# A 256-node graph network: one-hots of the last layer moved behind the next sums' remainder, a new order of the first stage, attention keys made as rows, fillers near the end

## What is computed

```python
x = _layernorm(x + _L0_gnn_ref(...))   # relational conv (3 relations) + gate over queries, twice
x = _layernorm(x + _L1_gnn_ref(...))   # plain graph conv
x = _layernorm(x + _L2_gnn_ref(...))   # relational attention, 4 heads, then 1 head
x = _layernorm(x + _L3_gnn_ref(...))   # relational conv, 34 relations, then a graph conv

# gate of the first layer: what the first stage prepares
qg = jnp.einsum('blf,gf->blg', q, Wg[:, F:]) + bg
# attention of the third layer
xr = jnp.einsum('nd,rdf->rnf', x, W)
qi = xr[etype, dst] @ q
kj = xr[etype, src] @ k
alpha = jax.nn.leaky_relu(qi + kj, NEG_SLOPE)
# last layer
mean = agg.reshape(N_REL, n, -1) / jnp.maximum(cnt, 1.0).reshape(N_REL, n, 1)
h1 = jnp.einsum('rni,rio->no', mean, W_rel) + x @ W_root + b_rgcn
```

## Time and profile before

| | us |
|---|---|
| median of three runs | 1136.41 (1133.11 to 1136.69) |
| the profiled execution, its time | 1134.0 |
| the profiled execution, its span | 1132.3 |
| PE busy in the span | 1078.2 (95%) |
| DVE busy | 768.5 (68%) |
| ACT busy | 572.1 (51%) |
| POOL busy | 179.9 (16%) |

### The profile page before, as it was taken

The page is one execution under the profiler, slowest core; times in us unless marked ns, Lnnn a source line. Parts: engine busy times, 40 slices in busy tenths (PEclk is TensorE's granted clock), DMA queues, the critical chain, the costliest instruction groups (busy, mean ns, idle before and its releaser), DMA issues.

```text
span 1132.3 us, 17627 instructions
## 1 busy us (share of the span) xinstructions
PE 1078.2 (95%) x7440; PEld 894.1 (79%) x7440; DVE 768.5 (68%) x1082; ACT 572.1 (51%) x602; POOL 179.9 (16%) x96
## 2 busy tenths in 40 slices
PE   7999999999999999999999889899999999999987
PEld 5899986545699965457689889759999999999974
DVE  6993855888743158885364665557788888888852
ACT  0433225888433268883233544225666656666630
POOL 2334702555100025551000000000000000000000
PEclk9999999999999999999999899999999999999999
DMA  9034276111044381120244004409777777777720
GB/s 295 11 99 154 85 235 197 57 57 57 1 167 168 121 241 57 57 57 3 93 157 167 29 1 168 163 1 320 244 238 246 248 252 242 248 234 248 241 85 28
DMA packets 82323, 163.47 MB, mean 144 GB/s; under 512 B 4035, under 2 KB 60127, under 8 KB 81951
## 3 DMA queue, kind: packets, MB, share of 16 engines
q1 hardware_dynamic: 80736, 151.86, 39.8%
q0 software_dynamic: 1504, 10.44, 3.6%
HBM read 158.64 MB, written 0.80 MB: 141 GB/s over the span
## 4 chain that ended last, share of the span: by engine, by line
PE 68%; DVE 19%; ACT 5%; issue 4%; DMA 1%; POOL 1%; SPq 0%; DVEq 0%; ACTq 0%; POOLq 0%
PE PS L1012 12%; PE PS L714 7%; PE PS L870 7%; PE PS L730 5%; PE PS L461 4%; PE PS L636 4%; DVE Wlo L1822 3%; PE PS L612 3%; PE PS L1026 3%; PE PS L995 3%; PE PS L474 3%; ACT Whi L1346 3%; PE PS L543 2%; PE PS L770 2%; PE PS L931 2%
## 5 line engine op out<-in xcount | busy, mean ns | idle before, releaser
L1822 DVE TENSOR_TENSOR Wlo<-W,Whi 128x2304 fp32r<-128x2304 f32 x68 | 173.7, 2556 | 43.5 <-ACT Whi L1346 43.4
L1346 ACT CAST Whi<-W 128x2304 fp32r<-128x2304 f32 x68 | 144.4, 2125 | 0.0
L1012 PE MATMUL PS<-Whi,Mhi 128*128 128x384 f32 x408 | 139.6, 342 | 3.5 <-DVE Mlo L1851 3.5
L1012 PE MATMUL PS<-Wlo,Mhi 128*128 128x384 f32 x408 | 136.6, 335 | 0.0
L1012 PE MATMUL PS<-Whi,Mlo 128*128 128x384 f32 x408 | 136.5, 335 | 0.0
L433 POOL TENSOR_TENSOR PRDP<-arena 128x1024 f32<-128x1024 f32 x48 | 114.6, 2388 | 113.7 <-PE PS L730 86.5
L714 PE MATMUL PS<-QH,SEL 128*128 128x512 f32 x384 | 115.7, 422 | 5.2 <-ACT xT L1186 1.4
L1207 ACT ACTIVATE arena<-PS 128x1024 f32<-128x1024 f32 x96 | 98.5, 1026 | 23.5 <-PE PS L714 23.5
L714 PEld LDWEIGHTS PS<-QH,SEL 128*128 128x128 f32 x384 | 64.8, 188 | 55.1 <-DVE PRD L1592 21.3
L1207 ACT ACTIVATE PS<-PS 128x1024 f32<-128x1024 f32 x96 | 97.9, 1020 | 2.6 <-PE PS L714 2.6
L1012 PEld LDWEIGHTS PS<-Whi,Mhi 128*128 128x128 f32 x408 | 76.7, 188 | 8.3 <-DVE Mlo L1851 8.3
(11 more groups left out here) (276 smaller groups left out, 2391.4 us busy)
## 6 DMA issues: line engine op xcount, KB each, us to landing
W<-in_L_rel SPq DMA_DIRECT2D x68, 1152.0 KB, 5.8
W<-in_W_rel SPq DMA_DIRECT2D x6, 2304.0 KB, 8.5
W<-in_W SPq DMA_DIRECT2D x6, 2304.0 KB, 8.5
arena<-in_qU SPq DMA_DIRECT2D x96, 128.0 KB, 2.6
W<-in_WqT SPq DMA_DIRECT2D x4, 2304.0 KB, 9.8
W<-in_W_root SPq DMA_DIRECT2D x2, 2304.0 KB, 13.6
W<-in_WgT SPq DMA_DIRECT2D x2, 2304.0 KB, 9.0
QH<-QH POOLq DMA_DIRECT2D x2, 1536.0 KB, 10.4
```

The lines of the kernel that those rows point to most:

```text
L1012: mm = pe.matmul(PS[:, 4 + s % 2, 0:HALF], MS[a][mb][:, k, j * P:(j + 1) * P], WS[b][w % 3][:, k, :], start=n == 0, stop=n == 17)
L1346: nc.scalar.copy(WS[0][w % 3][:], W[(FIRST34 + r) % 2][:, :, q * HALF:(q + 1) * HALF]).then_inc(w_hi, 1)
L1822: V.tensor_tensor(WS[1][w % 3][:], W[(FIRST34 + r) % 2][:, :, q * HALF:(q + 1) * HALF], WS[0][w % 3][:].bitcast(F32), ALU.subtract).then_i ...
```

## The change

It has four parts. First, in the last layer, the one-hots with `j = 1` are made in s = 0 of the pair behind the remainder of part 2, not in s = 3 ahead of it. Second, the first stage: the bias comes from eight matmuls in the rounded format with 33 rows (`BG` holds the rounded bias in row 0 and its remainder in row 32, `ROWS2` ones in these rows); ACT and POOL make `BG` and `ROWS2`; the first half of the query product comes ahead of the counts; relation 2 is counted behind the halves; and DVE's list is put in another order. Third, `queries_keys` holds `qk1` as weights (8 columns) and streams 256 columns of the transposed tiles, DVE negates rows into `qkR`, `spread_keys` spreads a row of it, and `turn_queries` turns the rows into `qkN`; `turn_rows(2)` comes ahead of `queries_keys(1)`. Fourth, `keep_busy(12, 7)` stands behind the `pe.Else` block.

```diff
@@ tensor engine, first stage @@
-            pe.wait_ge(consts, 2)
-            pe.wait_ge(bg_in, 16)
-            for at in range(4 * 3):
-                pe.matmul(PS[:, at // 2, (at % 2) * THIRD:(at % 2 + 1) * THIRD], ones[0:1, :],
-                          biasN[0:1, 5, at % 3 * THIRD:(at % 3 + 1) * THIRD], start=at % 2 == 0, stop=False, skip_group_check=True)
+            pe.wait_ge(bg_ready, 1)
+            for u in range(2):
+                for bank, at, f, n in ((0, 0, 0, 512), (1, 0, 512, 256), (1, 256, 0, 256), (2, 0, 256, 512)):
+                    pe.matmul(PS[:, 3 * u + bank, at:at + n], ROWS2[:], BG[:, f:f + n], start=at == 0, stop=False,
+                              skip_group_check=True)
+            pe.wait_ge(q_in[0], 16)
+            for q in range(3):
+                pe.wait_ge(w_in[0] if q == 2 else first_in[q], 16)
+                mm = natural3(qT[0], W[0], last=True, thirds=[q])
+            mm.then_inc(q_done, 1)
             for c in range(EC):
...
@@ tensor engine, attention @@
-                for t in range(NT):
-                    at = (t * R3 + r) * 2 * HEADS1
-                    for k in range(KC):
-                        mm = pe.matmul(PS[:, 3, at:at + 2 * HEADS1], XT[:, r, k, t * P:(t + 1) * P], qk1[:, k, :],
-                                       start=k == 0, stop=k == KC - 1)
-                return mm
+                for k in range(KC):
+                    mm = pe.matmul(PS[0:2 * HEADS1, 3 + r // 2, (r % 2) * NODES:(r % 2 + 1) * NODES], qk1[:, k, :], XT[:, r, k, :],
+                                   start=k == 0, stop=k == KC - 1)
+                mm.then_inc(qk_done, 1)
+
+            def turn_queries():
+
+                for c in range(R3 * NT):
+                    r, t = divmod(c, NT)
+                    mm = pe.transpose(PS[:, 6, 2 * HEADS1 * (R3 * t + r):2 * HEADS1 * (R3 * t + r + 1)],
+                                      qkR[:, c * P:(c + 1) * P], ident[0:2 * HEADS1, 0:2 * HEADS1])
+                mm.then_inc(rows_turned, 1)
...
+                    for r in range(R3 if l == 0 else 0):
+                        mm = pe.matmul(PS[:, 4 - h % 2 * 2 + r // 2, (r % 2) * NODES:(r % 2 + 1) * NODES],
+                                       ident[0:2 * HEADS1, HEADS1 + h:HEADS1 + h + 1].to_broadcast([2 * HEADS1, P]),
+                                       qkR[:, r * NODES:(r + 1) * NODES], start=True, stop=True)
@@ tensor engine, end @@
+            keep_busy(12, 7)
             to_turned(4, hN, ready=lambda t: pe.wait_ge(h1_copied, t + 1)).then_inc(h_turned, 1)
@@ gpsimd, first stage @@
+            pool.wait_ge(consts, 2)
+            pool.wait_ge(bg_hi, 2)
+            nc.gpsimd.tensor_tensor(BG[32:33, :], biasN[32:33, 5, :], BG[32:33, :].bitcast(F32), ALU.subtract).then_inc(bg_ready, 1)
@@ vector engine, attention @@
-                    dve.wait_ge(qk_done, 1)
-                    V.tensor_scalar(qkN[:], PS[:, 3, 0:NT * R3 * 2 * H].rearrange("p (t r h) -> p t r h", t=NT, r=R3),
-                                    -1.0, None, ALU.mult).then_inc(qkn_copied, 1)
+                    dve.wait_ge(qk_done, 2)
+                    V.tensor_scalar(qkR[:, 0:2 * NODES], PS[0:2 * H, 3, :], -1.0, None, ALU.mult).then_inc(qkr_copied, 1)
+                    dve.wait_ge(qk_done, 3)
+                    V.tensor_scalar(qkR[:, 2 * NODES:], PS[0:2 * H, 4, 0:NODES], -1.0, None, ALU.mult).then_inc(qkr_copied, 1)
+                    dve.wait_ge(rows_turned, 1)
+                    V.tensor_copy(qkN[:], PS[:, 6, 0:NT * R3 * 2 * H].rearrange("p (t r h) -> p t r h", t=NT, r=R3)
+                                  ).then_inc(qkn_copied, 1)
@@ vector engine, last layer @@
                         if s == 0 and p:
                             sums_lo(p, 2)
+                            if p + 1 < PAIRS34:
+                                pair_onehots(p + 1, 1)
...
-                        elif p + 2 < PAIRS34:
-                            pair_onehots(p + 2, s - 2)
+                        elif s == 2 and p + 2 < PAIRS34:
+                            pair_onehots(p + 2, 0)
```

More of the change, by code:

```diff
@@ L133, in build @@
         qkN = sb("qkN", [P, NT, R3, 2 * HEADS1])
+        qkR = put("qkR", [2 * HEADS1, R3 * NODES], F32, 36)
         RC = sb("RC", [P, 2, NODES])
@@ L375, in _ @@
             nc.gpsimd.tensor_copy(iotab[:], iota1[:]).then_inc(consts, 1)
-            pool.dma_start(biasN[:, 5, :], A["bg"].partition_broadcast(P)).then_inc(bg_in, 16)
+            pool.dma_start(biasN[0:33, 5, :], A["bg"].partition_broadcast(33)).then_inc(bg_in, 16)
+            then(nc.gpsimd.memset(ROWS2F[:], 0.0))
+            then(nc.gpsimd.memset(ROWS2F[0:1, :], 1.0))
+            nc.gpsimd.memset(ROWS2F[32:33, :], 1.0).then_inc(rows2_set, 1)
+            pool.wait_ge(rows2_set, 1)
             then(nc.gpsimd.iota(relid[:], pattern=[[1, R34]], base=0, channel_multiplier=0,
@@ L577, in _ @@
                     mm.then_inc(cnt_summed, 1)
-            pe.wait_ge(q_in[0], 16)
-            for q in range(3):
-                pe.wait_ge(w_in[0] if q == 2 else first_in[q], 16)
-                mm = natural3(qT[0], W[0], last=True, thirds=[q])
-            mm.then_inc(q_done, 1)
+            pe.wait_ge(e_ready, R3)
+            pe.wait_ge(half_read, 1)
+            for s in range(NT):
+                for c in range(EC):
+                    mm = pe.matmul(PS[:, 6, s * NODES:(s + 1) * NODES], S1[:, c, s * P:(s + 1) * P], E[0][:, c, :],
+                                   start=c == 0, stop=c == EC - 1)
+            mm.then_inc(cnt_summed, 1)
+            pe.wait_ge(consts, 2)
             pe.wait_ge(cnt_copied, 2)
@@ L587, in _ @@
             mm.then_inc(deg_spread, 2)
-            counts(2, 0, bank=6)
             pe.wait_ge(q_in[1], 16)
@@ L904, in spread_keys @@
                         pe.wait_ge(score_done, u0 + 2 * h - 2)
-                    for c in range(R3 * NT):
+                    for r in range(R3 if l == 0 else 0):
+                        mm = pe.matmul(PS[:, 4 - h % 2 * 2 + r // 2, (r % 2) * NODES:(r % 2 + 1) * NODES],
+                                       ident[0:2 * HEADS1, HEADS1 + h:HEADS1 + h + 1].to_broadcast([2 * HEADS1, P]),
+                                       qkR[:, r * NODES:(r + 1) * NODES], start=True, stop=True)
+                    for c in range(R3 * NT if l == 1 else 0):
                         r, s = divmod(c, NT)
@@ L936, in _ @@
                     spread_keys(h)
+                    if l == h == 0:
+                        turn_queries()
                 keep_busy(30 if l == 0 else 52, 7)
@@ L1121, in third_hi_first @@
                 nc.scalar.copy(WH[(w + 1) % 3][:], third_turned(W[m % 2], w % 3)).then_inc(wr_hi, 1)
-            act.wait_ge(cnt_summed, 1)
-            third_hi_first(0)
-            third_hi_first(1)
+            act.wait_ge(rows2_set, 1)
+            nc.scalar.copy(ROWS2[:], ROWS2F[:]).then_inc(bg_hi, 1)
+            act.wait_ge(bg_in, 16)
+            nc.scalar.copy(BG[:], biasN[0:33, 5, :]).then_inc(bg_hi, 1)
             for t in range(NT):
@@ L1128, in _ @@
                 if t == 0:
+                    third_hi_first(0)
+                    third_hi_first(1)
                     act.wait_ge(x_in, 32)
@@ L1446, in _ @@
             dve.wait_ge(chunk_ready, EC)
+            then(V.scalar_tensor_tensor(out=ekey[:, 0, :], in0=keyf[:, 2, :], scalar=2.0, in1=keyf[:, 1, :], op0=ALU.is_equal, op1=ALU.mult))
+            onehot(E[0], ekey[:, 0, :]).then_inc(e_ready, R3)
             for h in range(2):
@@ L1453, in _ @@
                 then(V.scalar_tensor_tensor(out=low, in0=high, scalar=-STEP, in1=both, op0=ALU.mult, op1=ALU.add))
+                dve.sem_inc(half_read, 1)
             V.tensor_tensor(CNT[:, 0], CNT[:, 0], NRM[:, 1], ALU.add).then_inc(cnt_copied, 1)
             V.tensor_tensor(CNT[:, 1], CNT[:, 1], NRM[:, 2], ALU.add).then_inc(cnt_copied, 1)
-            then(V.scalar_tensor_tensor(out=ekey[:, 0, :], in0=keyf[:, 2, :], scalar=2.0, in1=keyf[:, 1, :], op0=ALU.is_equal, op1=ALU.mult))
-            onehot(E[0], ekey[:, 0, :]).then_inc(e_ready, R3)
-            onehot(E[1], keyf[:, 1, :]).then_inc(d1_ready, 1)
             def normalise_counts(n):
```

22 lines of the change are left out of this document (15 added, 7 removed).

## The result

The changed kernel takes **1117.5 us** (median of 4 runs, 1116.7 to 1119.2), the kernel before on the same chip 1135.3 (4 runs, 1133.1 to 1136.7): ratio 0.984, 95% interval 0.981 to 0.987. The forecast was 1122.5 with a range from 1117.5 to 1128, so the sign held and so did the mechanisms of the last layer and the first stage, while the attention was priced wrongly: 17.8 us were gained where 12.7 were forecast. The profiled execution of after took 1118.25 us against 1134.0, and has 15.8 of these 17.8.

A forecast was written before the change was run, and what follows sets the result against it. PE was taken to bound the last layer, PE and DVE the first stage, a DVE and ACT chain the attention. First stage -4.5, attention -1.7, last layer -7.0, fillers +0.5: -12.7 from 1135.2, so 1122.5 us, range 1117.5 to 1128.

The forecast's parts named there:

- Last layer, forecast -7.0: Last layer: moved one-hots let `Mlo` come 0.72 us earlier, ending PE's stall; 0.47 x 15 = 7.0 us gained.
- The 0.04 a pair: Last layer: average loss counted per pair because `Ylo` is next to be late, with 0.1 to 0.15 us left.
- the first rival: Last layer: `Ylo` binds instead, by 0.25 us or more a pair; layer gains 3.8, time 1125.7 us; chance 0.15.
- First stage, forecast -4.5: First stage: DVE decides and `Tlo` starts at 81.3, 4.4 us earlier; gain rounded to 4.5 us.
- PE's -5.3: First stage, PE: bias -10.6, new bias and later start +2.5, half clock level paid by the query product +2.8.
- Attention, forecast -1.7: Attention: scores start earlier, by the middle of 2.8 and 0.8 us, rounded down to 1.7.
- If half a relation and half the spread fall in it, 1.3 + 0.7 are lost: Attention: loss from PE's lower clock level, leaving 0.8 us of the 2.8 us gain.
- The reading that a busy PE keeps its clock: Attention: by the Trainium skill's page the relations keep the upper level; term -2.8, time 1.1 us lower.
- raised the level by 1.2: Whole kernel: base put at 1135.2 us, halfway between the profiled 1134.0 and the runs' median, 2.4 above it.
- Fillers, forecast +0.5: End: twelve fillers cannot fill the gap, cost 1.35 us, and give 0.7 to 1.0 back in the product; net +0.5.
- The third rival: All parts at their good ends: -6 - 2.8 - 7.6 - 1.2 = -17.6, time 1117.6 us; chance 0.10.
- The fifth rival: Last layer: `Ylo` late in every pair; at 0.6 further behind, 9 us lost, time 1138.5 us; chance 0.03.

The follow-up runs named there:

- e11: The changed kernel with the one-hots of the last layer in their old place; 1125.6 us, ratio 0.990 to the kernel before.
- e5: The changed kernel with all eight one-hots of a pair behind the next sums' remainder, ahead of `Ylo`; 1130.4 us, ratio 0.994 to the kernel before.
- e1: The kernel before with only the last layer's one-hots with j = 1 moved; 1127.4 us, ratio 0.990 to the kernel before.
- e2: The kernel before with the attention's part alone; 1133.2 us, ratio 0.996 to the kernel before.
- e3: The kernel before with the first stage's part alone; 1134.3 us, ratio 0.998 to the kernel before.
- e10: The changed kernel with the attention's order and query sums as before; 1125.8 us, ratio 0.990 to the kernel before.
- e4: The changed kernel without the twelve filler matmuls behind the Else block; 1119.3 us, ratio 0.984 to the kernel before.

## Why the prediction missed

**Last layer, forecast -7.0, measured -7.7** (6.8 by medians). Every step stood: the wait of `half_product` for `Mlo` is gone, it returns with the one-hots (e11), and `Ylo` is what comes next. The 0.04 a pair taken off for it was not lost. e5 shows how near the first rival was: 0.72 us more at this place cost 0.70 a pair.

**First stage, forecast -4.5, measured -4.9 at `Tlo`** (4.2 to 5.4, mean 4.9, in nine other executions with the new stage), and -5.6 where the gates begin, since PE waited 0.6 less for a transfer ahead of them. In e1 and e2, with the old stage, the gates begin 1.7 and 1.6 later than in the profile of before, so that one was on the good side here as well; on average over three executions with the old stage and ten with the new one the gates come 7.0 sooner. The engine that decides, DVE, was right, as were its pieces: 6.75 for `E0`, 37.99 for the start of its list, 0.69 for the product that had met POOL. PE's -5.3 was right too, by its first later product (63.2, 5.5 earlier). The timed runs of e3 show less (-2.7 by the ratio, interval -0.9 to -4.5, and -1.7 by the medians). In its trace the attention is 3.0 slower than in the profile of before, by the clock, and the end 3.2, of which 2.8 are the second gap.

**Attention, forecast -1.7, measured -2.7 against the profile of before, -4.8 in the traces on average: the term that failed.** By the times it is -2.8 to -4.4 alone (e2) and -7.0 when it is undone (e10, with the second gap). Two steps of it were wrong. First, "If half a relation and half the spread fall in it, 1.3 + 0.7 are lost": nothing of it was. In each of eleven executions the phase took the 12.7 of the sum of pieces. The bias matmuls, busy throughout with one row of 128 at 1.2 GHz, were the wrong relative; they follow an idle PE, these follow full products, and that this is the reason is argued, not tried. The margin was small: the fall did come, 1.6 us behind the scores' start in the changed kernel and at that start in e2. The reading that a busy PE keeps its clock, which the prediction had set beside it at -2.8, would have been right for this execution. Second, and worth more, the size of the old phase: "Now the phase lasts from 619.06 to 634.52, 15.5 us" is one execution, and a lucky one. In three others it is 18.3 to 19.7, so against these the phase gains 6.1 (mean 18.8 less 12.7), against all four 5.3. Behind it DVE and ACT's chain gives a little back: from the first matmul of `rows` to the first turned probabilities the old code takes 64.1, 68.4, 67.1 and 66.9 us, the new one 61.5 in nine of eleven executions (the others 63.1 and 63.2), 4.8 less on average. The rows themselves had a warning: the earlier trace rows show relation 3 at 2.88 and then the spread at twice its price, so the clock fell in the middle of the phase, and where it falls need not be the same each time. The forecast raised the level by 1.2 for the runs and put none of it where it belonged.

The old attention and a slow end go together. From the last scatter to the last product it takes 28.7, 29.7 and 31.9 us with the old attention and no fillers (before, e1, e3), 27.2 and 26.7 with the new one (e2, e4). In e3 the second gap accounts for 2.83 of it; without that the five are 28.7, 29.7, 29.1 and 27.2, 26.7, so about 2.2 us remain. They are in the product, which takes 17.87 to 18.30 in the first three, where the granted clock is 0.50 for 6.8 to 10.2 us ahead of it and in it, and 15.72 in the other two, where it is 0.50 for 3.4. Why that should hang on the attention is not shown; it stays open.

**Fillers, forecast +0.5, measured about +1.9.** That they stand behind the gap and can't fill it was right; that the product recovers by them was not. The product takes 15.72 with them and 15.72 without (e4), and the step that priced them at 1.35 us assumed the upper level, where they ran at the lower one (2.74). In the seven executions with the whole new attention and the twelve fillers the end takes 28.3 to 29.6 us, mean 28.9, against 27.0 for e2 and e4. Timed runs can't separate it (1119.3 without; 1117.5 and 1118.8 with).

**The sum.** By the traces: first stage -5.6, attention -4.8, the faster end that goes with it -2.2, last layer -7.7, fillers +1.9: -18.4, where -17.3 and -17.8 were measured (with the first stage's average of -7.0 it would be -19.8); averages over a few executions leave that much open. Of the 5 us by which the forecast was short, the attention makes 3.1 and the end that goes with it 2.2; the other terms, -1.1, -0.7 and +1.4, nearly cancel. The third rival, everything at the good ends, gave 1117.6 and had a chance of 0.10; that it met the time is luck, since its parts are wrong (an attention at -2.8, fillers that save 1.2). The fifth rival's price holds a slip: at 0.38 us behind its point the time is just 1135.2, and it takes 0.6 to be 0.3% above. Nothing else hangs on it.

## What to carry to other kernels

A phase in which TensorE works at less than its full array differed here by 4 us between executions with the same code; profile such a phase more than once before a term is sized against it, and compare medians with medians. An instruction moved past a stall has to be priced at its new place to the tenth of a microsecond: here 0.72 us were free and 1.44 us cost more than the stall had. Whoever makes an engine earlier must look at what it releases: twice a gain on PE or DVE was lost because a POOL subtraction then ran beside DVE's one-hots. And a changed part can go together with a gap at a place that has nothing to do with it, as the old query sums did near the end: look at the gaps marked issue before a difference is put down to the part itself.
